# The value product of an attention tile follows its transposed scores by four tiles instead of two

## The reference

```python
q = (x @ Wq).reshape(b, n, h, dh).transpose(0, 2, 1, 3)
k = (x @ Wk).reshape(b, n, h, dh).transpose(0, 2, 1, 3)
v = (x @ Wv).reshape(b, n, h, dh).transpose(0, 2, 1, 3)
dots = jnp.einsum('bhnd,bhmd->bhnm', q, k) * SCALE
top_dots, top_inds = jax.lax.top_k(dots, TOPK)
attn = jax.nn.softmax(top_dots, axis=-1)
out = jnp.einsum('bhnk,bhnkd->bhnd', attn, vg)   # vg: the rows of v at top_inds
return out.transpose(0, 2, 1, 3).reshape(b, n, h * dh) @ Wo + bo
```

## Time and profile before

| | us |
|---|---|
| median of 3 runs | 9320.89 |
| their lowest and highest | 9319.95, 9331.5 |
| the profiled execution | 9336.33 |
| its span, first to last instruction | 9334.6 |

### The profile page before, as it was taken

The page is one execution under the profiler, slowest core; times in us unless marked ns, Lnnn a source line. Parts: engine busy times, 40 slices in busy tenths (PEclk is TensorE's granted clock), DMA queues, the critical chain, the costliest instruction groups (busy, mean ns, idle before and its releaser), DMA issues. The chain is left out here.

```text
span 9334.6 us, 604193 instructions
## 1 busy us (share of the span) xinstructions
PE 8227.5 (88%) x266349; PEld 4441.4 (48%) x266732; DVE 5465.7 (59%) x15245; ACT 3963.6 (42%) x7646; POOL 1955.6 (21%) x2042
## 2 busy tenths in 40 slices
PE   3899999999998779478759999999999999999998
PEld 2677777777776667367632222222222222222222
DVE  4677777777776447533245555555555555555554
ACT  3455555555554335144424343444343444343443
POOL 0555555555555235100000000000000000000000
PEclk9999999999999889689869999999999999999999
DMA  0000000000000000000000000000000000000000
GB/s 36 1 0 0 0 0 0 0 0 0 0 0 0 0 0 0 2 1 0 30 11 1 3 3 3 1 3 3 3 3 3 1 3 3 3 3 3 1 3 5
DMA packets 9761, 32.01 MB, mean 3 GB/s; under 512 B 1525, under 2 KB 3130, under 8 KB 9274
## 3 DMA queue, kind: packets, MB, share of 16 engines
q1 hardware_dynamic: 9274, 26.02, 0.7%
HBM read 17.63 MB, written 8.39 MB: 3 GB/s over the span
## 5 line engine op out<-in xcount | busy, mean ns | idle before, releaser
L1932 DVE MAX8 w_best<-psum 128x8 f32<-128x128 f32 x8192 | 1724.4, 283 | 1289.5 <-PE psum L1465 1244.0
L1915 ACT ACTIVATE w_exp<-psum 128x512 f32<-128x512 f32 x2048 | 1221.0, 596 | 2387.0 <-PE psum L1474 2384.7
L1484 PE MATMUL psum<-w_exp,w_v 128*32 128x512 f32 x4096 | 2096.1, 610 | 1.0 <-ACT w_inverse L1517 1.0
L499 PE MATMUL psum<-e_prod_u,e_j 32*32 32x64 f32 x49152 | 769.4, 216 | 30.3 <-ACT e_prod_u L579 25.1
L499 PEld LDWEIGHTS psum<-e_prod_u,e_j 32*32 32x32 f32 x49152 | 707.6, 106 | 182.5 <-issue 182.5
L1474 PE MATMUL psum<-w_q,w_k 99*128 99x512 bf16 x2048 | 789.8, 386 | 1.4 <-ACT w_q L1499 1.4
L1465 PE MATMUL psum<-w_k,w_q 96*128 96x512 bf16 x2048 | 628.0, 389 | 156.2 <-DVE w_best L1932 114.0
L1484 PEld LDWEIGHTS psum<-w_exp,w_v 128*32 128x32 f32 x4096 | 277.0, 108 | 757.2 <-issue 757.2
L653 POOL TENSOR_TENSOR e_diag<-odd,e_eye 128x512 f32<-128x512 f32 x384 | 488.2, 1271 | 561.7 <-PE psum L473 523.6
L547 ACT ACTIVATE e_square<-e_off 128x512 bf16<-128x512 f32 x384 | 242.0, 630 | 844.2 <-POOL e_off L657 844.2
L1465 PEld LDWEIGHTS psum<-w_k,w_q 96*128 96x128 bf16 x2048 | 121.5, 97 | 993.4 <-issue 990.0
(11 more groups left out here) (282 smaller groups left out, 11628.4 us busy)
## 6 DMA issues: line engine op xcount, KB each, us to landing
odd<-in_x SPq DMA_DIRECT2D x1, 8192.0 KB, 23.3
even<-in_x SPq DMA_DIRECT2D x1, 8192.0 KB, 23.6
out<-w_t SPq DMA_DIRECT2D x16, 512.0 KB, 2.6
w_hid<-in_fc SPq DMA_DIRECT2D x2, 256.0 KB
w_wo<-in_wo SPq DMA_DIRECT2D x8, 8.0 KB
w_wq<-in_wq SPq DMA_DIRECT2D x1, 64.0 KB
w_wk<-in_wk SPq DMA_DIRECT2D x1, 64.0 KB
w_wv<-in_wv SPq DMA_DIRECT2D x1, 64.0 KB
```

Source lines behind the costliest of these rows:

```text
L499: last = nc.tensor.matmul(halves(e.pair[:, k // HALF, :])[rows, :, to], e.j[rows, cols], e.prod_u[rows, :, cols], start=True, stop=True)
L1484: nc.tensor.matmul(banks[7][slot(j), :], w.v[:, kt, 4 * g + j, :], w.exp[x % 4][:], start=(kt == 0), stop=(kt == KT - 1)).then_inc(s.weigh ...
L1915: nc.scalar.activation(w.exp[x % 4][:], banks[4 + x % 2], ACT.Exp).then_inc(s.exp_done, 1)
L1932: last = nc.vector.max(w.best[:, i, o, :], banks[o // 4][:, P * (o % 4):P * (o % 4) + P])
```

## The change

The distance between a tile's transposed scores and its value product becomes a constant, LAG, of 4 where it was 2, and the number of exponential buffers becomes a constant, EXPS, which stays 4. On TensorE the order in an iteration becomes: transposed score 2i, value product 2i-4, the work beside, transposed score 2i+1, value product 2i-3. Iterations 0 and 1 have no value products, and after the loop come value products 28, 29 and 30, then the turning of the maxima and value product 31. ScalarE's waits keep their meaning: exponential x waits for value product x-4.

```diff
+EXPS = 4
+LAG = 4
@@ class Tiles
-        self.exp = [sb(f"w_exp{n}", [P, QB]) for n in range(4)]
+        self.exp = [sb(f"w_exp{n}", [P, QB]) for n in range(EXPS)]
@@ weigh_pe
-        nc.tensor.matmul(banks[7][slot(j), :], w.v[:, kt, 4 * g + j, :], w.exp[x % 4][:], start=(kt == 0),
+        nc.tensor.matmul(banks[7][slot(j), :], w.v[:, kt, 4 * g + j, :], w.exp[x % EXPS][:], start=(kt == 0),
                          stop=(kt == KT - 1)).then_inc(s.weighed, 1)
@@ phase_pe
-                if weighs and x >= 2:
-                    weigh_pe(pe, before, unit, x - 2, not closes)
+                if weighs and x >= LAG:
+                    weigh_pe(pe, before, unit, x - LAG, not closes)
                 if x % 2 == 0 and i >= 1 and scored:
                     beside_pe(pe, b, phase, i, back, front)
         if weighs:
-            weigh_pe(pe, before, unit, 30, not closes)
+            for x in range(32 - LAG, 31):
+                weigh_pe(pe, before, unit, x, not closes)
@@ phase_act
-                    if closes or x >= 4:
-                        act.wait_ge(s.weighed, before * 32 + (x - 3))
-                    nc.scalar.activation(w.exp[x % 4][:], banks[4 + x % 2], ACT.Exp).then_inc(s.exp_done, 1)
+                    if closes or x >= EXPS:
+                        act.wait_ge(s.weighed, before * 32 + (x + 1 - EXPS))
+                    nc.scalar.activation(w.exp[x % EXPS][:], banks[4 + x % 2], ACT.Exp).then_inc(s.exp_done, 1)
```

## The result

The changed kernel takes 9428.73 us in the median (9421.65 to 9434.36) against 9326.15 (9319.95 to 9331.5) in the runs beside it: a ratio of 1.0110, with a 95% interval of 1.0092 to 1.0127, some 103 us more. The forecast was 9353 with a range of 9300 to 9400: the direction is right, the size is too small, and the measured time lies outside the range. The profiled execution took 9424.67 us with a span of 9422.9, and its mean granted clock is 0.944 where it was 0.954.

The account below looks back on a forecast made before the run. TensorE bounds most iterations, VectorE some. From the profiled 9336.3 us, minus 10.5 (54.5 gained at i=1, 44 lost to late exponentials), plus 43 for the clock: 9368.8, as a median 9353, range 9300 to 9400.

Parts of the forecast that it names:

- The wait of the exponential: Attention loop: from a phase's fifth on, each exponential starts 0.98 us later, behind value product x-4; TensorE keeps 1.0 us slack.
- The case that the loop would be bound by it: Rival, phases 1 and 3: the delay overruns the stack copy's slack; 0.2 us overrun costs 72 us, 9425; chance 0.12.
- the case that the exponentials are not late: Rival: buffers come free early or ScalarE's wait costs nothing, so 44 us fall away; 9266 or 9300; chance 0.08.
- The late places: Phase 1 i=8, phase 2 i=14, phase 3 i=2: late exponentials pass on 0.98 us each, 15 times, 44 us.
- The end of the phase: Ahead of each turning: four value products together lie inside TensorE's wait for VectorE's maxima; cost 0.
- The gain at i=1: Two value products leave i=1: phase 0 gains 19 us, phase 1 17, phase 2 16.5, phase 3 0; together 54.5.
- the case that the order gains nothing: Rival at i=1: VectorE bound it already, 44 us remain as loss, 9365 before the clock; no chance of its own.
- The clock: TensorE falls to half clock around new or longer idle gaps at four places: 43 us taken, bounds 0 to 89.
- Phase 3, i=1: TensorE idles some 2.8 us before score 2; falls expected in two of three: 15 us taken, 0 to 23.
- Phase 0: Clock at i=1: a new 1.3 us gap lets half clock last into the next iterations; 15 us taken, 0 to 20.
- End of phase 2: Clock: the gap before the turning grows from 2.82 to 3.80 us; 10 us taken, 0 to 23.
- the clock stays as it is: Rival: the new gaps bring no change of clock, only the 10.5 us gain is left, 9310; chance 0.24.

Follow-up runs that it names:

- the filled kernels: Unused extra TensorE products put into idle gaps: of the kernel before, 9304.97 us (0.9973 of it unfilled); of the changed kernel, 9332.06 us (1.0008 of the kernel before).

## Why the prediction was wrong in size

**The wait of the exponential: right.** Predicted were exponentials that start right behind the value product ahead of them and a loop that doesn't feel it. They start 0.10 us behind it, and the iteration stays at 3.03 us. The case that the loop would be bound by it fell: over all 15 images TensorE waits 17.7 us for ScalarE's copy of a stack, in 15 waits, one an image at i=1 of phase 1. So did the case that the exponentials are not late.

**The late places: right, in place and price.** Taken were 3 x 0.98 x 15 = 44 us; phase 1 i=9, the end of phase 2 and phase 3 i=3 lost 1.04, 1.03 and 1.04, 47 us, and two buffers at distance 2 show the same three by themselves.

**The end of the phase: right.** Four value products stand together ahead of the turning and cost nothing of their own: with six buffers the way from score 15 of phase 2 to the turning is 5.91 us, before it was 5.92. There the four take 1.06 us together (the x8 row above), as long as two in the earlier trace rows. In the changed kernel they take 1.60 us at the end of phase 2 and 3.30 us of idle time follow (timeline):

```profile
6694.11 1.60 PE L1486 MATMUL psum<-w_exp,w_v 128*32 128x512 f32 x8
...
6699.01 1.05 PE L1493 MATMUL psum<-w_ident,w_shift 128*3 128x128 bf16 x16 [3.30 <-DVE w_shift L1535]
```

I had expected 3.8 us of gap. Product 30 has to wait for its own late exponential and starts 0.6 us behind the other three, which shortens the gap by 0.5 us.

**The gain at i=1: near as a sum by luck, wrong in part.** The sum is 57 us against 54.5, and phases 1 and 2 are as read, so the case that the order gains nothing fell. But the 1.66 us of phase 0 are no gain of the order. The 1.65 of the earlier trace rows was measured in an iteration at half clock; the filled kernels of before and at distance 4 show 3.02 and 2.57 there, 0.45 us. The rest of the work at half clock was not saved, it was pushed into the next iteration, where 2.21 us came back. My own text noted that 13 passes are at half clock and two gain only 0.4; in the trace 11 of the 15 are at half clock and four take 3.02 us. I should have taken 0.45 for all and have had the clock's price in that phase separately. So counted the order gains 39 us, not 54.5, which is less than the 47 of the late exponentials: even without the clock the sum of 10.5 us faster was wrong in sign.

**The clock: the step that failed.** It was taken at 43 us, at most 89, and measured at 106, or 88 without what belongs to the gain that wasn't one. For the 14 images the 88 are 82 us, half of the 164 us that TensorE spent more at half clock. By place:

- Phase 3, i=1: taken 15 (0 to 23), measured 43. Both factors were wrong. The gap brought a fall in all images, not in two of three; and a fall costs 2.89 us there on the mean, not 1.52. I took the 1.52 us from one way behind a turning and made it the upper bound of every fall. Of the ten falls behind that turning in the kernel before, three had cost 2.7 to 2.8 us, such as this one:

```profile
7226.24 1.87 PE L1491 MATMUL psum<-w_ident,w_shift 128*3 128x128 bf16 x16 [2.83 <-DVE w_shift L1533]
...
7232.69 0.60 PE L1465 MATMUL psum<-w_k,w_q 96*128 96x512 bf16 x2
```

  That is 6.45 us of way against 3.74, so 2.71 for a fall behind the same gap. The stretch at 0.50 in the earlier trace rows is this very image. The better bound was in that row: of 6.60 us at half clock TensorE is busy for 5.66. If work takes half as long at full clock, up to 2.83 us are lost wherever TensorE sets the pace; in the changed kernel's phase 3 it is busy for 5.93 of 6.60, which gives 2.97. By this estimate that place reaches to 2.83 x 15 = 42 us, and with 2.71 x 15 = 41 for the end of phase 2 the bounds sum to 126, not 89; 9310+126 = 9436 would have held the measured time.
- Phase 0: taken 15, measured some 35 (+0.14 and +2.21 an image), of which 18 are the other side of the gain that wasn't one (1.66-0.45 = 1.21 an image).
- Phase 1: taken 3, measured 8, at i=2.
- End of phase 2: taken 10, measured 4. The way behind that turning grew from 4.95 to 5.23 only: falls came in 13 of 14 images instead of 9, but each cost 1.6 us and none 2.7.
- Phase 2, i=13 and 14: not foreseen, 15 us, in a place where the change opens no new gap. Timeline of the changed kernel and the stretch behind it:

```profile
6684.38 1.92 PE L1281 MATMUL psum<-w_mean_column,w_squares 128*128 128x1 f32 x16
...
6686.46 1.86 PE L1486 MATMUL psum<-w_exp,w_v 128*32 128x512 f32 x2
```

```profile
6686.60:6689.90 3.30, 3.30 (x6) 0.46 (x5) 0.47 (x3) 0.60 (x1) 0.00 (x0) 0.50 0.00 0
```

  Ahead of the fall stand 16 products of a single column and only 0.12 us more idle time than before. No experiment was aimed at it, but the two parts of the change bear on it: at i=13 or 14 a fall begins in 9 of 14 images of the changed kernel, in 6 with the late exponentials alone (two buffers, distance 2), in 2 with the distance alone (six buffers) and in 1 before. Why it falls there stays open.

Common to these points is the assumption that falls are independent chances that follow from the length of each gap. They aren't: the gap of 2.8 us brought one in 9 of 14 images before and in 2 of 14 with six buffers at distance 4. The reading under it, that gaps of 1.95 us brought none, was wrong as well: the turning of phase 3 behind such a gap is slow in three images of the kernel before. From turning to turning of phase 3, twelve of 13 images of the changed kernel take 286.5 to 286.9 us, those of before 277.4 to 281.9. In the changed kernel a fall stands in phase 0 and in phase 3 of every image, and one more at phase 1 i=2 in five images and at phase 2 i=13 in the other nine, never at both. With one gap filled, falls were more costly elsewhere (phase 1 i=2, above). That the period of the image locks onto the falls would fit all this; no run tested it.

**The page cited.** By the rule of the Trainium skill (TensorE: Matmul & The Clock Gate, section Why this matters for your kernels), which warns only of idle gaps longer than this one, the phase 3 term would have been zero. The trace disagrees: behind 2.66 us of gap 0.50 is granted in 14 of 14 images, in 13 from inside the gap on, and with the gap filled in none.

**The rivals.** Of the case "the clock stays as it is" nothing holds. What it would have been is shown by the filled kernels: the change is 28 us slower, with some falls left, and not 10.5 faster.

## What to carry to other kernels

Moving TensorE's work out of an iteration that another engine bounds gains nothing there and opens a gap. Price a gap not by its idle time but by what stands behind it: by the estimate above a fall of the clock costs up to half of TensorE's busy time in the stretch that the trace shows at 0.50. The length of a gap alone does not tell whether a fall comes; the same 2.8 us brought one in 9 of 14 images of one kernel and in 2 of 14 of another. When a consumer (here the value product) moves back by as many places as there are buffers, the producer's next write waits for the product right ahead of it: give it two buffers more, or move it one place less. Where a few idle gaps of 2 to 3 us recur, throw-away products that end before the next real one is due are worth a try, and a count that is too high delays what it stands before.

## What the runs showed of the hardware

- TensorE fell to half clock around a gap of 2.66 us every time (14 of 14 images), around one of 1.68 us at the same place in none of 14 (in one of 14 with other gaps filled), and around one of 1.36 us never; 12 throw-away products of 96x512 in it (2.75 us) took the fall away and 26 to 36 us off the kernel.
- Whether a gap brings a fall is not a matter of its length alone: behind the gap of 1.95 us at the end of phase 3 the turning is slow in 3 of 14 images before, in none with distance 4 and four buffers, and in all 14 with six buffers. The effects of two edits don't add up: 0.10% and 0.59% alone, 1.10% together.
- Value products of different column groups that follow each other run side by side: two take 1.05 us (x4) and four 1.06 (x8, with six buffers), while one that alternates with a transposed score holds TensorE for 0.98 by itself. That is why products moved to the end of a phase cost nothing there.
- A duration read at half clock is not the duration of that place: 4.26 us at phase 0 i=1 were 3.02 with the gap ahead of it filled.
